# First expert stage: gathered rows read in 128-byte pieces, turned by VectorE's 32x32 block transpose, and output weighted by ScalarE

## What is computed

```python
x = x + y @ wo.T                                      # attention, residual
flat = _rmsnorm(x, ln2_w).reshape(-1, Cx)             # (8192, 128)
probs = softmax(flat @ router_w.T)
tp, ti = top_k(probs, 2); tp = tp / (sum(tp) + 1e-09)
for e in range(8):                                    # HID = 341
    hh = silu(flat @ w1[e].T) * (flat @ w3[e].T)      # (n, 341)
    out = out + weights[:, e:e + 1] * (hh @ w2[e].T)
```

## Time and profile before

| | us |
|---|---|
| median of three runs | 1493.25 |
| lowest and highest run | 1490.9, 1496.06 |
| profiled execution, span | 1492.9 |
| first experts, first to last matmul | about 613 to 905 |
| one tile of 256 rows in the middle of the stage | 4.15 |

### The profile page before, as it was taken

How to read it: one execution, slowest core, us unless ns; L and a number is a source line. 1 busy time by engine, 2 the same in 40 slices (tenths; PEclk the granted TensorE clock), 3 DMA queues, 4 the chain that set the end, 5 groups by cost and what they waited for, 6 DMA issues and landing times. The chain is left out here.

```text
span 1492.9 us, 32014 instructions
## 1 busy us (share of the span) xinstructions
PE 1180.9 (79%) x8595; PEld 1004.2 (67%) x8595; DVE 1029.2 (69%) x3960; ACT 742.6 (50%) x1864; POOL 869.1 (58%) x742
## 2 busy tenths in 40 slices
PE   5888888767888772599999994666775089999996
PEld 3666656557878772488888883545554079989995
DVE  3788888999888874367777765667775435565554
ACT  5777777546676772133333331434443035555553
POOL 3466666552556777344444442245776748887887
PEclk9999999979898995799999997879777579999999
DMA  7300000000000111466666664233421225545553
GB/s 188 54 2 2 2 1 2 2 1 1 30 30 32 39 41 57 141 196 196 196 196 196 196 209 138 84 93 92 122 94 60 78 50 72 71 63 71 71 69 45
DMA packets 126249, 122.53 MB, mean 82 GB/s; under 512 B 16576, under 2 KB 108096, under 8 KB 126128
## 3 DMA queue, kind: packets, MB, share of 16 engines
q1 hardware_dynamic: 92720, 85.65, 20.4%
q0 software_dynamic: 32960, 35.36, 12.0%
q10 hardware_dynamic: 448, 0.10, 0.0%
HBM read 76.71 MB, written 44.34 MB: 81 GB/s over the span
## 5 line engine op out<-in xcount | busy, mean ns | idle before, releaser
L2866 POOL DMA_INDIRECT out<-m_yb,m_dsti x142 | 228.4, 1608 | 64.3 <-DVE m_yb L2966 26.9
L2160 POOL DMA_INDIRECT rows<-m_yb,m_dsti x135 | 129.2, 957 | 169.5 <-DVE m_dsti L2291 147.9
L1384 POOL DMA_INDIRECT dispatch<-g_flat,g1r_pos x128 | 129.4, 1011 | 76.0 <-issue 32.3
L2236 ACT ACTIVATE m_sg<-psum 128x256 f32<-128x256 f32 (+3 forms) x216 | 79.8, 370 | 178.7 <-PE psum L2189 174.8
L1126 POOL DMA_INDIRECT dispatch<-common_v,a1r_pos x128 | 129.3, 1010 | 54.3 <-issue 35.5
L2939 ACT ACTIVATE m_hT<-psum,m_w 128x256 f32<-128x256 f32 (+1 forms) x240 | 92.8, 447 | 100.7 <-PE psum L2893 99.8
L2189 PE MATMUL psum<-m_xT,m_w 128*128 128x256 f32 (+3 forms) x648 | 140.3, 366 | 0.7 <-ACT m_xT L2227 0.7
L2189 PEld LDWEIGHTS psum<-m_xT,m_w 128*128 128x128 f32 (+1 forms) x648 | 106.2, 178 | 18.3 <-ACT m_xT L2227 0.9
L2904 PE MATMUL psum<-m_w,m_hT 128*128 128x128 f32 x848 | 104.7, 275 | 3.1 <-DVE m_yb L2962 3.1
L2893 PE MATMUL psum<-m_xT,m_w 128*128 128x256 f32 (+1 forms) x480 | 104.9, 363 | 1.0 <-issue 0.8
L2904 PEld LDWEIGHTS psum<-m_w,m_hT 128*128 128x128 f32 x848 | 99.4, 192 | 3.7 <-issue 2.8
(11 more groups left out here) (316 smaller groups left out, 3219.4 us busy)
## 6 DMA issues: line engine op xcount, KB each, us to landing
m_w<-in_c_wall SPq DMA_DIRECT2D x54, 533.0 KB
ahead_w<-in_c_wall SPq DMA_DIRECT2D x18, 533.0 KB, 4.2
g1c_y<-rows SPq DMA_DIRECT2D x32, 256.0 KB, 3.4
m_xg<-dispatch SPq DMA_DIRECT2D x47, 132.0 KB
m_xg<-dispatch SPq DMA_DIRECT2D x46, 130.0 KB, 2.2
resident<-in_c_wall SPq DMA_DIRECT2D x8, 578.0 KB, 6.0
out<-x SPq DMA_DIRECT2D x16, 256.0 KB, 5.9
out<-m_yb,m_dsti POOLq DMA_INDIRECT x142, 3.3
```

What stands on the lines that cost most here:

```text
L1384: pool.indirect_dma_start(out=dest, out_offset=bass.IndirectOffsetOnAxis(ap=self.pos[t % 2][:, k, p:p + 1], axis=0), in_=flat[:, p, :], in ...
L2160: pool.indirect_dma_start(out=rows_out, out_offset=bass.IndirectOffsetOnAxis(ap=dsti[j][:, t:t + 1], axis=0), in_=yb[j][:, t, :], in_offse ...
L2236: act.activation(sg[j % 2][0:cn, k, 0:rows], up_banks[j % 2][k][0:cn, 0:rows], ACT.Silu)\
L2866: pool.indirect_dma_start(out=out_rows, out_offset=bass.IndirectOffsetOnAxis(ap=dsti[j][:, t:t + 1], axis=0), in_=yb[j][:, t, :], in_offse ...
```

## The change

Rows of a tile no longer come in one DMA with one row per partition. `load_blocks` reads them with five DMAs: four of them each put one 32-column strip of all rows (pieces of 128 bytes) into 32 partitions, so that each 32x32 block lies where the transposed tile needs it; a fifth reads the four tags (16 bytes a row) into a small tile `tag`. One VectorE instruction (`turn`) then transposes every 32x32 block of `xb` into `xr`, which is the transposed tile; it replaces TensorE's `x_T` and its PSUM bank. ScalarE still multiplies by `ln2_w` into `xT`, now from SBUF, and takes over `out`: two activations of 128 columns with the share as scale instead of one VectorE instruction. VectorE reads the tags from `tag`. A tile's load counts six DMAs instead of two.

```diff
@@ Ahead.sync
         for t in (LAST_BATCH - 1, LAST_BATCH):
             R.wait_landed(sp, t)
+        if wall is not None:
+            load_blocks(sp, rows_in, at, 2, self.xb, self.tag, self.loaded[name])
+            return
         sp.dma_start(self.xg[:, :, 0:rows_in.shape[-1]], rows_in.rearrange("(a p) c -> a p c", p=HALF)[bass.ds(at, 2), :, :].rearrange("a p c -> p a c"))\
...
+LOADS = 6
...
+def load_blocks(sp, rows, at, n, blocks, tags, loaded):
+    b = rows.rearrange("(a b j) c -> a b j c", b=4, j=32)[bass.ds(at, n), :, :, :].rearrange("a b j c -> j (a b) c")
+    for q in range(4):
+        sp.dma_start(blocks[32 * q:32 * q + 32, 0:n, :].rearrange("j a (b i) -> j (a b) i", i=32), b[:, :, 32 * q:32 * q + 32]).then_inc(loaded, 16)
+    sp.dma_start(tags[:, 0:n, :], rows.rearrange("(a p) c -> a p c", p=HALF)[bass.ds(at, n), :, C:ROW].rearrange("a p c -> p a c")).then_inc(loaded, 16)
...
@@ phase_experts, sync
                     n = halves(g, j)
-                    sp.dma_start(xg[j][:, 0:n, :], list_halves[bass.ds(at, n), :, :].rearrange("a p c -> p a c")).then_inc(loaded[j], 16)
+                    load_blocks(sp, rows_in, at, n, xb[j], tag[j], loaded[j])
@@ phase_experts, tensor
-                def x_T(g, j):
...
-                    for t in range(halves(g, j)):
-                        i = pe.transpose(bT[:, 128 * t:128 * t + 128], xg[jj][:, t, 0:C], ident[:, :])
-                    i.then_inc(pe_x.sem, 1)
                 def up(g, j):
+                    here(pe, g, j)
                     pe.wait_ge(*xT_ready.now(g, j))
...
-                        if not (last and j == n - 1):
-                            x_T(g, j + 1)
@@ phase_experts, scalar
                 def x_T(g, j):
-                    act.wait_ge(*pe_x.now(g, j))
+                    act.wait_ge(*turned.now(g, j))
...
+                def out(g, j):
+                    jj = j % UN
+                    act.wait_ge(*pe_down.now(g, j))
+                    act.wait_ge(*share_ready.now(g, 6 * j + 5))
+                    for t in range(halves(g, j)):
+                        i = act.activation(yb[jj][:, t, :], bY[:, 128 * t:128 * t + 128], ACT.Copy, scale=share[jj][:, t:t + 1])
+                    i.then_inc(y_ready.sem, 1)
...
                         if not (last and j == n - 1):
                             x_T(g, j + 1)
+                        if not (first and j == 0):
+                            out(g, j - 1)
@@ phase_experts, vector
-                    dve.tensor_tensor(yb[jj][:, 0:n, :], src, bass.AP(v.tensor, v.offset, [v.ap[0], [1, n], [0, C]]), ALU.mult)\
-                       .then_inc(y_ready.sem, 1)
+                def turn(g, j):
+                    jj = j % UN
+                    gg = g + 1 if j == UN else g
+                    here(dve, gg, jj)
+                    dve.wait_ge(*xT_ready.now(g, j - 2))
+                    n = halves(gg, jj)
+                    dve.transpose(xr[j % 2][:, 0:HALF * n], xb[jj][:, 0:n, :].rearrange("r t c -> r (t c)")).then_inc(turned.sem, 1)
...
+                        if not (last and j == n - 1):
+                            turn(g, j + 1)
                         if adds:
                             late_add(g, j)
```

More of the change, by code:

```diff
@@ L2079, in phase_experts @@
         w = [ahead.w] + [sb(f"w{i}", [128, NW]) for i in range(1, UN)]
-        xg = [ahead.xg] + [sb(f"xg{i}", [128, 2, ROW]) for i in range(1, UN)]
+        xb = [ahead.xb] + [sb(f"xb{i}", [128, 2, C]) for i in range(1, UN)]
+        tag = [ahead.tag] + [sb(f"tag{i}", [128, 2, ROW - C]) for i in range(1, UN)]
+        xr = [sb(f"xr{i}", [128, TILE]) for i in range(2)]
         yb = [sb(f"yb{i}", [128, 2, C]) for i in range(UN)]
@@ L2091, in phase_experts @@
         stored = [raw(f"stored{i}") for i in range(UN)]
[L2092 removed]
+        pe_up, pe_down = sig("pe_up", UN * NK), sig("pe_down")
+        turned = sig("turned")
         xT_ready, act_done = sig("xT_ready"), sig("act_done", UN * NK)
@@ L2170, in _ @@
             def _(pe):
-                open_signals(pe, [pe_x, pe_up, pe_down])
-                def x_T(g, j):
[L2174 to L2177, removed]
-                    for t in range(halves(g, j)):
-                        i = pe.transpose(bT[:, 128 * t:128 * t + 128], xg[jj][:, t, 0:C], ident[:, :])
-                    i.then_inc(pe_x.sem, 1)
+                open_signals(pe, [pe_up, pe_down])
                 def up(g, j):
+                    here(pe, g, j)
                     pe.wait_ge(*xT_ready.now(g, j))
@@ L2202, in down, with body @@
                     i.then_inc(pe_down.sem, 1)
-                def body(g, first=False, last=False):
-                    n = tiles_in(g)
-                    for j in range(n):
+                def body(g, first=False):
+                    for j in range(tiles_in(g)):
                         up(g, j)
-                        if not (last and j == n - 1):
-                            x_T(g, j + 1)
                         if not (first and j == 0):
                             down(g, j - 1)
-                x_T(0, 0)
                 body(0, first=True)
@@ L2215, in _ @@
                 for g in range(LIKE, TURNS):
-                    body(g, last=g == TURNS - 1)
+                    body(g)
                 down(TURNS - 1, LAST - 1)
@@ L2220, in _, with body @@
             def _(act):
-                open_signals(act, [xT_ready, act_done])
+                open_signals(act, [xT_ready, act_done, y_ready])
                 def x_T(g, j):
-                    act.wait_ge(*pe_x.now(g, j))
+                    act.wait_ge(*turned.now(g, j))
                     act.wait_ge(*pe_up.now(g, NK * (j - 2) + NK - 1))
                     rows = HALF * halves(g, j)
-                    act.activation(xT[j % 2][:, 0:rows], bT[:, 0:rows], ACT.Copy, scale=scale[:, 0:1]).then_inc(xT_ready.sem, 1)
-                def body(g, last=False):
+                    act.activation(xT[j % 2][:, 0:rows], xr[j % 2][:, 0:rows], ACT.Copy, scale=scale[:, 0:1]).then_inc(xT_ready.sem, 1)
+                def out(g, j):
[5 more added lines that the diff above has]
+                    i.then_inc(y_ready.sem, 1)
+                def body(g, first=False, last=False):
                     n = tiles_in(g)
@@ L2262, in late_add, with body @@
                     dve.tensor_tensor(xt, xt, late[:, bass.ds(g * UN + j, 1), :], ALU.add)
-                def body(g, first=False, adds=True):
-                    for j in range(tiles_in(g)):
+                def body(g, adds=True, last=False):
+                    n = tiles_in(g)
+                    for j in range(n):
                         rows = HALF * halves(g, j)
+                        if not (last and j == n - 1):
+                            turn(g, j + 1)
                         if adds:
@@ L2307, in row_share @@
                     dve.tensor_tensor(out_, out_, sum_, ALU.mult).then_inc(sr.sem, 1)
[L2309 to L2314, removed]
+                turn(0, 0)
+                body(0)
                 body(1)
@@ L2317, in _ @@
                 for g in range(LIKE, TURNS):
-                    body(g, adds=g < PAIRS // UN)
-                stored_before(TURNS - 1, LAST - 1)
-                out(TURNS - 1, LAST - 1)
+                    body(g, adds=g < PAIRS // UN, last=g == TURNS - 1)
         clear_taken(nc)
```

38 lines of the change are left out of this document (16 added, 22 removed).

## The result

The changed kernel takes 1546.72 us (median of four runs, 1543.77 to 1547.72); the kernel before took 1494.24 beside it. The ratio is 1.0353, with an interval of 1.0335 to 1.0371: slower by 52.5 us. The forecast was 1541 us, with a range of 1522 to 1568.

A forecast was written before the change was run, and what follows sets the result against it. TensorE, never resting in the first expert stage, bounds the kernel; SyncE's 150.8 us of added issue, less 101.4 of waits and 1.2 given back, adds 48.2 to 1492.9: 1541 us, range 1522 to 1568.

The forecast's parts named there:

- SyncE's room of 101.4 us: SyncE's 67 waits for `y_ready` in the first expert stage, to take up 150.8 us of added issue; 49.4 remain.
- the signs that it named: In the stage: few `y_ready` waits, DMAs 0.53 us apart, pace 4.7, TensorE busy 3.93, idling on loads, DMA share near 0.7.
- full tile on SyncE: SyncE's need per full tile: 2.58 + 2.12 = 4.70 us, above TensorE's 3.93, so SyncE sets the pace.
- from one strip to the next: Start-to-start distance of the added DMAs on SyncE's queue: 0.53 us, with 0.47 and 0.57 as ends.
- half tile: SyncE's 9 half tiles: four added DMAs of 0.48 us each, 17.3 us together; a half tile takes 2.58 + 1.92.
- on the way to the first matmul: The load ahead of the stage: four added DMAs of 0.53 us, 2.1 us more.
- last load, given back: At the stage's end, the last load is used 3.3 us after issue; the usual landing is 2.1, giving back about 1.2.
- stage: First expert stage: 150.8 us more issue less 101.4 us of waits and 1.2 given back, 48.2 us longer.
- TensorE's saving, where SyncE lets it show: Two transposes fewer per full tile: 0.22 us of 4.15, 13.9 us in all, expected to go into TensorE's waiting.
- Slow pieces: Rival: at 44 ns a packet the transfers set the pace, 5.43 us a full tile, 1586 us; chance 0.09.
- Cheap issue: Rival: 32-partition DMAs at 0.34 us or less on SyncE, TensorE keeps the pace, 1479 us, faster; chance 0.06.
- More stalls: Rival: SyncE's DMA stalls come more often, 0.60 us a DMA, 70 us more, 1563 us; chance 0.10.

The follow-up runs named there:

- the run with the pieces alone: Kernel before, rows read in 128-byte pieces by only two more DMAs a tile, TensorE still turning rows: 1498.11 us, ratio 1.0017.

## Why the prediction was right

Its main step was that SyncE's room of 101.4 us is too small for four more DMAs a tile, so that SyncE becomes the engine that sets the pace. The trace has the signs that it named, but for one: no wait for `y_ready`, DMAs about half a microsecond apart, TensorE's idle time handed down from the loads, a DMA share of 0.72. The one that it lacks: TensorE was to be busy for about 3.93 us of a tile, and is for 201.73 / (228 / 4.72) = 4.18; in the tiles shown above 1.53 - 1.34 = 0.19 us of the difference are an overlap that is lost. By its terms:

| step | forecast | measured |
|---|---|---|
| full tile on SyncE | 4.70 us | 4.72 (mean), 4.61 (the tile shown) |
| from one strip to the next | 0.53 us | 0.505 |
| half tile | 2.58 + 1.92 = 4.50 us | 4.39 |
| on the way to the first matmul | 2.1 us | 13.87 - 13.06 = 0.8 |
| last load, given back | 1.2 us | 3.3 - 2.0 = 1.3, then lost again |
| stage | + 48.2 us | + 47.0 |
| TensorE's saving, where SyncE lets it show | 0.22 us a tile | 0.20 and 0.22 |
| block transpose, 128x256 | 0.418 us | 0.445 |
| a packet of 128 bytes | 12 ns (44 at most) | 10 ns more |

Three of these need a word. The pace is right while the strip is cheaper than forecast, because the rest of SyncE's tile is dearer where most tiles are, in the hardware loop: 4.72 - 4 x 0.505 = 2.70 us against 2.58. That 2.70 is itself a mean. Over 13 turns of the loop the loads of weights lie 4.63, 4.59 and 4.53 us apart, and 5.11 from the last tile of a turn to the first of the next, as from 742.63 to 747.77. Tiles that are written out need less: the first one takes 624.01 - 619.66 = 4.35 us from one load to the next, and took 616.56 - 614.25 = 2.31 before, which leaves 0.51 for each strip. The forecast's 2.58, a mean over the whole stage, lies between the two sorts.

The way to the first matmul cost less. From the stage's first load of weights, the last DMA of the first tile's list is issued after 8.54 us before and 10.62 now, 2.08 later as forecast; but that last DMA is the one of the tags, and its data are used 618.78 - 616.62 = 2.2 us after the issue, where it was 613.53 - 610.23 = 3.3. Before:

```profile
610.23 0.40 SPq L1507 DMA_DIRECT2D ahead_xg<-dispatch  x1
613.53 0.66 PE L2179 MATMUL psum<-ident,ahead_xg 128*128 128x128 f32 x2 [30.07 <-ACTq L104]
```

and now:

```profile
616.62 0.40 SPq L2076 DMA_DIRECT2D ahead_tag<-dispatch  x1
618.78 0.45 DVE L2277 STREAM_TRANSPOSE m_xr<-ahead_xb 128x256 f32<-128x256 f32 x1 [16.31 <-DMA ahead_tag<-dispatch]
```

And the end of the stage gave nothing back. The load's own part was right: the tags are issued at 948.75 and the transpose starts at 950.75, 2.0 us instead of the 3.3 of the earlier trace rows. But the timeline of the last tiles shows what replaced it:

```profile
942.84 1.56 PE L2201 MATMUL psum<-m_xT,m_w 128*128 128x128 f32 x12 [1.37 <-DMA m_tag<-dispatch]
...
948.75 0.35 SPq L2076 DMA_DIRECT2D m_tag<-dispatch  x1
...
950.75 0.31 DVE L2277 STREAM_TRANSPOSE m_xr<-m_xb 128x128 f32<-128x128 f32 x1 [1.88 <-DMA m_tag<-dispatch]
951.60 2.90 PE L2201 MATMUL psum<-m_xT,m_w 128*128 128x128 f32 x12 [0.85 <-DMA m_tag<-dispatch]
```

The last up-projection takes 2.90 us where the same one two tiles earlier took 1.56. The granted clock from 950 to 955 us is 0.50, the lower level; the forecast has no term for it. So one end of the stage came out 1.3 us shorter than forecast and the other 1.2 longer. That the two cancel, and the stage lies so near its forecast, is luck; the pace of the tiles, which makes most of the sum, is not.

The rivals. Slow pieces, 1586 us at 44 ns a packet: the run with the pieces alone shows 10 ns and no loss of time. Cheap issue, 1479 us: it decided at 0.36 us a DMA, and a strip takes 0.505. More stalls, 1563 us: the longest strip took 0.536 us, where one DMA before took 1.143:

```profile
L2075 SPq DMA_DIRECT2D m_xb<-dispatch x216: 316/326/536, 620.2 to 948.2; - x108
```

The forecast lies 5.7 us under the median, and the stage explains none of that: it was forecast 1.2 us too long. A part is a slip of reckoning. 1541 is a span, the 1492.9 of before and 48.2, and the 0.35 us between that span and a median of other runs was taken for what lies around a span; but wherever a run's time and span are both on record, the time is 1.8 to 2.2 us longer, as 1546.4 against 1544.6 here. The rest stands ahead of the stage, where the changed kernel's profile was 4.3 us later. That doesn't follow the change: in the ten profiles the stage's first load lies between 601.1 and 607.4 us, at 601.1 for the changed kernel with `out` on VectorE and at 606.4 for the kernel before with short pieces. The kernel before itself had medians of 1499.0 and 1496.8 us beside the experiments, where it had 1494.24 beside the changed one. What makes the earlier stages vary so was not studied.

## What to carry to other kernels

An engine that only issues DMAs has a pace of its own, and the profile's busy times don't show it: before splitting a load, add up its waits, and compare them with the number of DMAs added times the distance between two of them in the timeline. When the room isn't there, the same DMAs can go onto the queue of an engine that has some; here two of four were enough to turn 3.5% lost into 0.4 to 0.7% gained. Look at the first tile when doing so: six strips issued ahead of ScalarE's first copy held it up for 4.61 us here.

## What the hardware showed that was not expected

- **A DMA instruction's time on the queue doesn't follow its pieces or bytes.** 32 partitions x 8 pieces of 128 bytes took 0.326 us, 128 x 2 of 16 bytes 0.395, 128 x 4 of 128 bytes 0.373, 128 x 2 of 528 bytes 0.384. From start to start it is 0.505 us for a strip and 0.55 for the load of 533 KB of weights.
- **Short pieces cost little in this range.** Splitting 528 bytes into four of 128 and one of 16 added 10 ns of engine time per packet. The Trainium skill ("DMA: Bandwidth & Descriptors", "Specifications") gives 512 bytes as the least transfer for line rate; the trace agrees that shorter ones take more of the engines, from 54.2% to 70.4% for the same 37.4 MB, and shows that this can stay hidden.
- **VectorE's transpose of all 32x32 blocks of a 128x256 float32 tile takes 445 ns**, 311 for 128x128:

```profile
L2277 DVE STREAM_TRANSPOSE m_xr<-m_xb x54: 311/445/446, 624.7 to 950.8; 128x256 f32<-128x256 f32 x47, 128x128 f32<-128x128 f32 x7
```

- **TensorE's clock fell between late loads, but not each time.** In the changed kernel's profile it was busy for 24.85 of the 45 us from 920 to 965, and the granted clock was 0.83 and 0.75; before, at the same place in the program, it was 1.00 though TensorE also had pauses. The stretch with the last up-projection, first of the changed kernel and then of the one before with four tag DMAs more, with the stretch ahead of it:

```profile
945.00:950.00 5.00, 2.38 (x17) 2.34 (x17) 1.92 (x13) 1.49 (x5) 0.96 (x1) 0.89 0.56 142
950.00:955.00 5.00, 4.15 (x20) 3.89 (x20) 2.67 (x16) 1.49 (x5) 0.96 (x1) 0.50 0.08 26
...
945.00:950.00 5.00, 2.41 (x20) 2.16 (x19) 2.13 (x15) 1.35 (x5) 1.18 (x2) 1.00 0.58 150
950.00:955.00 5.00, 3.62 (x30) 3.46 (x31) 3.45 (x23) 1.31 (x5) 1.55 (x2) 1.00 0.08 28
```

The second had the same pauses, kept the upper level here and did its last up-projection in 1.54 us instead of 2.90. So late loads can cost more than their own delay, but these runs don't show when they do.
